# Second attention pass over the edges of a graph kernel: the edge's own rows are weighed on ScalarE instead of VectorE

## The reference, cut to what matters

```python
feat = (x @ W).reshape(n, h, c)                      # h = 4 heads, c = 64
e = al_s[src] + al_d[dst]                            # edges and loops
e = jnp.where(e > 0, e, NEG_SLOPE * e)
m = jax.ops.segment_max(e, dst, num_segments=n)
ee = jnp.exp(e - m[dst])
s = jax.ops.segment_sum(ee, dst, num_segments=n)
alpha = ee / (s[dst] + 1e-16)
out = jax.ops.segment_sum(alpha[:, :, None] * feat[src], dst, num_segments=n)
...
x = x + out                                          # then layernorm, relu, the next layer's query
```

## Time and profile before

| | us |
|---|---|
| median of 3 runs | 5303.44 |
| lowest, highest | 5288.44, 5304.99 |
| the profiled execution, its own time | 5288.36 |
| its span | 5286.6 |
| VectorE busy in the span | 4204.5 |
| TensorE busy | 4453.9 |
| ScalarE busy | 2974.0 |
| GpSimd busy | 3107.9 |

### The profile page before, as it was taken

The page is one execution under the profiler, slowest core; times in us unless marked ns, Lnnn a source line. Parts: engine busy times, 40 slices in busy tenths (PEclk is TensorE's granted clock), DMA queues, the critical chain, the costliest instruction groups (busy, mean ns, idle before and its releaser), DMA issues. The chain is left out here.

```text
span 5286.6 us, 75793 instructions
## 1 busy us (share of the span) xinstructions
PE 4453.9 (84%) x21191; PEld 3335.9 (63%) x21191; DVE 4204.5 (80%) x12564; ACT 2974.0 (56%) x7552; POOL 3107.9 (59%) x2813
## 2 busy tenths in 40 slices
PE   3999999999958888858888699999957757988887
PEld 3888888888736666636666456666634436765555
DVE  5999999999868888769999368888868878975554
ACT  2999999999914444414444357677745544431111
POOL 3676666666267676343333277777544426647777
PEclk9999999999979999968889899999978878999998
DMA  4888888888734444247777446555557766654444
GB/s 137 299 313 310 310 311 309 309 309 310 281 117 127 127 132 128 87 141 248 264 270 254 149 141 184 184 179 181 170 169 253 258 223 183 206 161 134 150 148 132
DMA packets 645561, 1096.74 MB, mean 207 GB/s; under 512 B 82230, under 2 KB 465654, under 8 KB 645021
## 3 DMA queue, kind: packets, MB, share of 16 engines
q1 hardware_dynamic: 525866, 837.50, 46.0%
q0 software_dynamic: 119168, 253.97, 16.1%
q10 hardware_dynamic: 112, 0.40, 0.0%
HBM read 523.88 MB, written 575.95 MB: 208 GB/s over the span
## 5 line engine op out<-in xcount | busy, mean ns | idle before, releaser
L1398 POOL DMA_INDIRECT got<-F,index x392 | 504.3, 1286 | 504.9 <-PE acc L1548 400.2
L850 PE MATMUL mm<-w,tt 128*128 128x264 f32 x3136 | 733.0, 387 | 2.6 <-ACT tt L894 2.6
L850 PEld LDWEIGHTS mm<-w,tt 128*128 128x128 f32 x3136 | 582.7, 191 | 93.1 <-ACT tt L894 2.8
L1557 ACT ACTIVATE rows<-acc 128x260 f32<-128x260 f32 (+1 forms) x588 | 227.4, 387 | 559.8 <-PE acc L1548 559.8
L1544 PE MATMUL acc<-got,sel 128*128 128x260 f32 (+1 forms) x1176 | 425.3, 449 | 99.2 <-DVE sel L1519 93.3
L816 POOL DMA_INDIRECT place<-PLACE,place_ix x392 | 413.3, 1054 | 119.4 <-issue 119.4
L2692 DVE SCALAR_TENSOR_TENSOR agg<-mask,agg,acc 128x128 f32<-128x128 f32 x784 | 247.9, 344 | 253.5 <-PE acc L2679 140.6
L850 PE MATMUL mm<-wl,tt 128*128 128x264 f32 x1568 | 411.7, 385 | 0.7 <-ACT tt L894 0.7
L788 POOL DMA_INDIRECT xd<-in_x_dram,index x196 | 224.6, 1146 | 316.7 <-DMA XD<-xd 285.1
L1287 PE MATMUL kv<-wkv,ht 128*128 128x512 f32 x784 | 378.4, 606 | 0.1
L1548 PE MATMUL acc<-rows,carry 128*128 128x260 f32 (+1 forms) x1008 | 349.2, 431 | 8.3 <-ACT rows L1557 1.9
(11 more groups left out here) (391 smaller groups left out, 13339.6 us busy)
## 6 DMA issues: line engine op xcount, KB each, us to landing
F<-f1o SPq DMA_DIRECT2D x97, 528.0 KB
F<-f2o SPq DMA_DIRECT2D x97, 528.0 KB
HL<-ho SPq DMA_DIRECT2D x97, 528.0 KB
xin<-in_x_dram SPq DMA_DIRECT2D x97, 512.0 KB, 5.8
H<-h SPq DMA_DIRECT2D x97, 512.0 KB, 3.3
X<-x3o SPq DMA_DIRECT2D x97, 512.0 KB, 3.5
out_dram<-oo SPq DMA_DIRECT2D x97, 512.0 KB
drow<-DSTF SPq DMA_DIRECT2D x84, 448.0 KB
```

Source lines behind the costliest of these rows:

```text
L850: last = nc.tensor.matmul(mm[PAIR[stage, q]][:, r, 0:F2W], lhs[:, q, 2 * r + k, :], w[:, k, :], start=(k == 0), stop=(k == KB - 1))
L1398: nc.gpsimd.indirect_dma_start(out=buf[:, n % SLOTS, t, :], out_offset=None, in_=table, in_offset=bass.IndirectOffsetOnAxis(ap=index[:, n ...
L1557: nc.scalar.activation(self.rows[:, n % 2, t, :], self.acc[tile % 2][:, 0:self.width], ACT.Copy)\
```

## The change

The product of the own rows leaves VectorE. ScalarE makes it instead: for each of the seven tiles four activations (Copy, 64 wide, one per head) with the own weight as a per-partition scale, 28 a group, each tile's four right behind `take_rows` of the same t. Note the two groups: `take_rows` works on b = n-1, `own_rows` on x = n-2. With tile 6 ScalarE raises the new semaphore `own`, and VectorE waits for it where its own two multiplications stood; the waits on fe, on the freed x1 buffer and on put move to ScalarE. The wait on den's order goes away with the two instructions. SyncE issues fe once `own` of the group before has been raised, and xe once x1 of the group before is there; each has a semaphore of its own, and VectorE waits for xe where it adds it.

```diff
@@ gat_output
                 if own is not None:
-                    for k in PIECES:
-                        last = V.tensor_tensor(by_head(o[:, k, :], H), by_head(own[:, k, :], H),
-                                               per_head(self.w_own(n)[:, k, :], D // H), ALU.mult)
-                    link(last)
+                    hold(dve, own, n + 1, None)
@@ SyncE
                         if within(x):
+                            hold(sp, d["own"], x, None)
+                            sp.dma_start(fe[:, :, :], edge_rows(F2, x, GS)[:, :, 0:D]).then_inc(fe_in, 16)
                             hold(sp, d["x1"], x, None)
-                            sp.dma_start(fe[:, :, :], edge_rows(F2, x, GS)[:, :, 0:D]).then_inc(fe_in, 16)
-                            sp.dma_start(xe[:, :, :], edge_rows(XD, x, GS)).then_inc(fe_in, 16)
+                            sp.dma_start(xe[:, :, :], edge_rows(XD, x, GS)).then_inc(xe_in, 16)
@@ VectorE
                             hold(dve, d["crow"], x + 1 if x == NS - 1 else x + 2, None)
-                            hold(dve, fe_in, 32 * (x + 1), None)
-                            hold(dve, x1_out[s], 16 * (x // 2), None)
-                            hold(dve, d["put"], x - 1, None)
-                            link(ph.gat_output(dve, link, x, row, den[:, :, :], fe[:, :, :]))
+                            link(ph.gat_output(dve, link, x, row, den[:, :, :], d["own"]))
                         if within(a):
                             ph.differences(dve, a)
                         if within(x):
+                            hold(dve, xe_in, 16 * (x + 1), None)
@@ ScalarE
+                    def own_rows(x, t):
+                        s = x % 2
+                        if t == 0:
+                            hold(act, d["wt"], x + 1, None)
+                            hold(act, fe_in, 16 * (x + 1), None)
+                            hold(act, x1_out[s], 16 * (x // 2), None)
+                            hold(act, d["put"], x - 1, None)
+                        for k in range(HQ):
+                            c = D // HQ
+                            last = nc.scalar.activation(x1[:, s, t, k * c:(k + 1) * c], fe[:, t, k * c:(k + 1) * c],
+                                                        ACT.Copy, scale=ph.w_own(x)[:, t, k:k + 1])
+                        if t == GS - 1:
+                            last.then_inc(d["own"], 1)
...
                         for t in range(GS + 2):
                             if within(b) and t < GS:
                                 ph.take_rows(act, b, t)
+                            if within(x) and t < GS:
+                                own_rows(x, t)
```

More of the change, by code:

```diff
@@ L1885, in gnn_program @@
         with SoftPass(HQ, 2, D + HQ, (F2, 7), None, H2) as ph:
-            ph.step("x1", "stats", "tp", "gt", "qm", "q", "chunks_turned", "chunk_sums", "sums_turned", "chunk_carry",
+            ph.step("x1", "stats", "own", "tp", "gt", "qm", "q", "chunks_turned", "chunk_sums", "sums_turned", "chunk_carry",
                     "carry_turned", "filled", "filled_turned")
@@ L1894, in gnn_program @@
             rt, nm = ph.sb("rt", [P, 2, GS]), ph.sb("nm", [P, 2, GS])
-            fe_in, x1_out, q_out = ph.sem("fe_in"), ph.slots("x1_out", 2), ph.slots("q_out", 2)
+            fe_in, xe_in, x1_out, q_out = ph.sem("fe_in"), ph.sem("xe_in"), ph.slots("x1_out", 2), ph.slots("q_out", 2)
             gt = ph.sb("gt", [P, 2, KB, P])
@@ L2071, in _ @@
                     ph.start_act(act)
+                    def own_rows(x, t):
[11 more added lines that the diff above has]
+                            last.then_inc(d["own"], 1)
                     def group(n):
-                        a, b, c, e = n, n - 1, n - 3, n - 4
+                        a, b, c, e, x = n, n - 1, n - 3, n - 4, n - 2
                         if within(e):
```

## The result

The changed kernel takes 5551.06 us (median of four runs, 5547.27 to 5556.83), the kernel before 5301.23 in the runs beside it: a ratio of 1.0477, interval 1.0456 to 1.0497. The forecast was 5550. Both profiled executions can be laid side by side: spans of 5551.5 and 5286.6 us, 264.9 apart.

What follows compares the result with a forecast made beforehand. Bound: two nearly equal loops, VectorE's list and TensorE-exponents-sel. Periods +233 and pass end +20 made +253 us on 5288.36, so 5541, stated as 5550 because the runs' median lay 15 us higher; range 5510 to 5620.

Steps and rivals of the forecast that it cites:

- What bounds the kernel: Second edge pass: VectorE's list and a loop through TensorE, ScalarE's exponents and VectorE's sel nearly equally long; period 22.98 us.
- The wait lands behind the row sums: ScalarE's list: own stands behind tile 6's row copy, so VectorE, asking at S+4, is answered after S+13.7 to S+15.2.
- S: The moment when VectorE's sel of a group ends; times within a group are counted from it in us.
- Price of a copy: ScalarE's 64-wide scaled copy: 332 ns long, 0.24 us start to start, 0.96 a tile, 6.7 a group.
- When own is done: ScalarE finishes a group's own rows at S+16.5 with a slow TensorE start, S+15.5 with a quick one; S+16.1 taken.
- What VectorE still has to do: From the row add after the wait to the end of the next sel: 16.1 us; period 16.1 + 16.1 = 32.2 us.
- The clock: TensorE idles longer before each group, so its granted clock in this pass falls (0.90 before), first work granted 0.50.
- The sum: Second edge pass: 24 periods of 32.2 plus 2 of 29.0, less 597.5: +233 us; pass end +20; total +253.
- The rule on shares: Skill's advice for saturated VectorE: by it alone 2.1 us a group come off, 54 us in all, giving 5249.
- Dearer copies: Rival: ScalarE's copies cost 0.40 us each, period 36.4, another +100, 5650 us; chance 0.05.
- Late transfers: Rival: fe, asked for only after own, lands too late; about 3 us a group, +80, 5630 us; chance 0.04.
- The hidden wait: Rival: own is already done when VectorE asks at S+4; hardly a gain, 5288 to 5303 us; chance 0.04.

Runs made afterwards that it cites:

- the store first: One group earlier, but SyncE sends the store of x1 right behind the load of xe, before waiting for own: 5320.38 us, ratio 1.004 to the kernel before.
- the wait alone: Kernel before, VectorE still multiplying, but first waiting for a ScalarE mark behind the row copy of tile 6; no copies: 5563.58 us, ratio 1.0511.
- the copies alone: Kernel before plus 28 ScalarE copies a group at the same place, on constants, read by nobody; VectorE still multiplies: 5303.71 us, ratio 1.0017.
- one group earlier: Changed kernel, but ScalarE makes own rows for group n-1 instead of n-2, and fe is loaded one group earlier: 5356.89 us, ratio 1.0116.

## Why the prediction was right, point by point

*What bounds the kernel.* That two loops were nearly equally long is borne out from both sides: taking 2.1 us off VectorE's gives nothing (the store first: period 23.41), shortening the other alone gives 0.9 us (22.10), both together 1.8 (21.22). The first is not quite clean, for the copies are added to the other loop there. The prediction named the exponents as the one place where VectorE meets the other loop; the differences, behind `turn_back`, are a second, and took the larger part (34.4 against 30.1 us in the store first).

*The wait lands behind the row sums.* Right, and shown: the wait alone gives 1.0511, the copies alone 1.0017, and own at S+10.9 in place of S+16.5 takes the period from about 32 to 26.9.

*Price of a copy.* 332 ns forecast, 337 measured, four in 1.05 us as reckoned. My figure of ScalarE busy near 20 us in 32 was wrong (17.3): I had summed lengths, where the column counts the overlap of neighbours once.

*When own is done.* S+16.5 in the group shown, as forecast for a slow start. The groups behind the first two average (3161.8 - 2392.05)/24 = 32.07 us; 32.2 was said. Less the 16.0 that follow, own comes near S+16.1 on the mean, as the sum took it. The two early periods were 27.6 and 28.4 in place of 29.0.

*What VectorE still has to do.* 16.1 forecast; 15.9 and 16.0 from L1572 to the end of sel.

*The clock.* TensorE's granted clock falls from 0.94 and 0.86 in the earlier trace rows to 0.76 and 0.77. It is 0.50 before the group shown, while TensorE waits for VectorE, and stays at 0.50 from 2714.3 to 2720, its first 6 us of work. In the group shown the row copy of tile 6 comes at the same S+15.2 as in the earlier trace rows, the group that started at the lower level.

*The sum.* +233 for the periods, measured +228; +20 for the end, measured +19.6. In the end two small errors cancel: the last group's own comes 1.9 us earlier than reckoned (S+42.4, not S+44.3), the two last loops take 0.9 longer (25.6, not 24.7). The rest, 17 us between the two profiled executions, was not in the forecast and lies in passes that the edit leaves alone; the number 5550 came out by adding 15 us for the quick profiled execution, which is about that rest. Between the medians lie 249.8 us, where +253 was forecast and 248 are found in the pass. That 5550 and 5551 meet within 1 us is luck; the agreement that counts is the one term by term.

*The rule on shares.* The Trainium skill, Perfetto Trace Analysis, section Optimizing Scalar/DVE Operations, says that moving work to ScalarE may make sense where VectorE is saturated. With the lists in order and the second loop shortened the move does pay here, 23 us (the prediction reckoned 54 by the rule alone), so the rule is not wrong for this kernel; it says nothing on the place, which decided.

*The rivals.* Dearer copies: excluded by 337 ns. Late transfers: fe lands in 4.7 to 5.3 us and nothing waits for it in the changed kernel; waits for transfers did appear once the copies were made a group earlier, first for the store of x1, then for fe. The hidden wait: not here, and when it was made (the store first) the result was indeed no gain, 5320 against 5300.

## What to carry to other kernels

Before work is moved to an idle engine, write down where in that engine's list it will stand and what its neighbours there wait for; if they wait for the engine that is to use the result, two halves that overlapped become a sum, however small the moved work is (here one 1-wide activation was enough). Work whose inputs are early can be placed one step of the pipeline earlier, but then its output buffer and its loads move earlier as well, and the waits in the DMA queue's list must be put in order again. An engine that is busy 93% of the time may still share its period with another loop; measure that one (by shortening it alone) before expecting the gain.

## What the runs showed of the hardware

A scaled copy of 64 columns takes 337 ns, and four stand 1.05 us: 0.24 us for each further one, less than half of the 0.40 us of a 259-wide one.

How long a transfer takes to land differed from kernel to kernel. All of these move seven tiles of 128 rows of 256 (896 KB); medians from 2400 to 2840 us, fe as load, x1 as store:

| | fe | x1 |
|---|---|---|
| kernel before | 5.0 | 11.2 |
| changed kernel | 5.0 | 8.4 |
| one group earlier | 5.5 | 9.8 |
| the store first | 10.0 | 8.8 |

In the groups looked at, SyncE has sent nothing for 12 us or more before fe in the first two kernels; in the third the load of xe goes out 3.1 us before it, in the last the store of x1 2.7 us. There fe takes twice as long. Whether the store is the reason was not tried.
